# Two-layer decoder on one Trainium2 core: the expert stages' second product as three fp32r products, routing weight applied per expert behind it

## The reference

```
h1 = einsum('bth,efh->btef', x, w1) + b1;  h1 = gelu(h1)
expert_outputs = einsum('btef,ehf->bteh', h1, w2) + b2
mixed_output = sum(topk_expert_outputs * topk_weights[..., None], axis=2)
```

```
h = relu(einsum('td,edh->teh', tokens, W1) + b1[None])
y = einsum('teh,ehd->ted', h, W2) + b2[None]
out = take_along_axis(y, expert[:, None, None], axis=1)[:, 0, :];  return out * max_prob
```

## Time and profile before

| | |
|---|---|
| median of 3 runs | 1724.21 us (1723.12 to 1724.45) |
| profiled execution: span | 1721.3 us |
| stage C, from its first bias product to the first work of stage D | 806.6 to 1030.1 us |
| stage F, from its first bias product to the last transposition of `yT` | 1595.1 to 1712.3 us |
| PE busy over the span | 1529.6 us (89%) |
| DVE busy | 1183.9 us (69%) |
| ACT busy | 959.5 us (56%) |
| POOL busy | 455.7 us (26%) |

### The profile page before, as it was taken

One profiled execution on the slowest core, in us unless ns is written; L12 is line 12 of the kernel. 1 busy time (PEld: TensorE's weight loads), 2 busy tenths in 40 slices (PEclk: granted clock), 3 DMA queues, 4 the chain that ended last, 5 costly groups with the idle time before them and its releaser, 6 DMA issues.

```text
span 1721.3 us, 22204 instructions
## 1 busy us (share of the span) xinstructions
PE 1529.6 (89%) x6864; PEld 893.3 (52%) x6864; DVE 1183.9 (69%) x3060; ACT 959.5 (56%) x1953; POOL 455.7 (26%) x385
## 2 busy tenths in 40 slices
PE   5899899999989979878999998999989897786997
PEld 3455455455544355444555555666655564453554
DVE  6988788788787264676755547666665766466675
ACT  4888688678788345543444435555454542353333
POOL 2455355445445221231000002222222221111000
PEclk9999999999999999998999999999999997898999
DMA  4000000000000030001000000000000000100000
GB/s 143 1 1 1 1 1 1 1 1 1 1 1 1 0 98 1 1 1 61 1 1 1 1 12 14 1 1 1 1 1 1 1 2 0 49 1 1 1 13 13
DMA packets 13508, 18.59 MB, mean 11 GB/s; under 512 B 832, under 2 KB 9808, under 8 KB 13264
## 3 DMA queue, kind: packets, MB, share of 16 engines
q1 hardware_dynamic: 12816, 16.06, 2.9%
q10 hardware_dynamic: 576, 1.11, 0.2%
HBM read 16.11 MB, written 1.05 MB: 10 GB/s over the span
## 4 chain that ended last, share of the span: by engine, by line
PE 64%; DVE 19%; ACT 9%; issue 6%; POOL 1%; DMA 0%; ACTq 0%; POOLq 0%; DVEq 0%
PE bank L625 8%; PE bank L445 7%; PE bank L377 6%; PE bank L435 4%; PE bank L428 3%; PE bank L760 3%; PE bank L506 3%; PE bank L549 3%; PE bank L520 2%; PE bank L726 2%; PE bank L756 2%; PE bank L608 2%; PE bank L610 2%; PE bank L609 2%; DVE work L1319 2%
## 5 line engine op out<-in xcount | busy, mean ns | idle before, releaser
L1771 POOL TENSOR_TENSOR work<-work 128x512 f32<-128x512 f32 x256 | 266.2, 1040 | 285.4 <-DVE work L1327 285.4
L1069 ACT ACTIVATE work<-bank,cols 128x512 f32<-128x512 f32 x192 | 131.8, 687 | 188.0 <-PE bank L610 187.3
L904 ACT ACTIVATE work<-bank,work 128x512 f32<-128x512 f32 x256 | 176.2, 688 | 103.9 <-DVE work L1319 102.6
L1555 DVE TENSOR_TENSOR work<-work,bank 128x512 f32<-128x512 f32 x192 | 130.1, 686 | 125.1 <-ACT work L1069 123.9
L1319 DVE TENSOR_REDUCE work<-bank 128x1 f32<-128x512 f32 x256 | 175.5, 686 | 42.2 <-PE bank L429 38.9
L625 PE MATMUL bank<-work,W 128*128 128x512 f32 x384 | 198.4, 600 | 4.4 <-DVE work L1555 4.4
L435 PE MATMUL bank<-cst,work 128*128 128x128 f32 x1024 | 157.1, 277 | 30.0 <-ACT work L912 26.5
L435 PEld LDWEIGHTS bank<-cst,work 128*128 128x128 f32 x1024 | 124.4, 142 | 80.2 <-issue 45.4
L428 PE MATMUL bank<-split 128*128 128x512 f32 x256 | 156.7, 612 | 1.8 <-ACT work L904 1.4
L912 ACT ACTIVATE work<-bank 128x512 f32<-128x512 f32 x256 | 151.2, 591 | 0.7 <-PE bank L435 0.3
L445 PE MATMUL bank<-work 128*64 128x512 f32 x512 | 139.0, 623 | 0.7 <-ACT work L912 0.7
(11 more groups left out here) (223 smaller groups left out, 3086.3 us busy)
## 6 DMA issues: line engine op xcount, KB each, us to landing
W<-in_w1T SPq DMA_DIRECT2D x1, 2048.0 KB, 8.1
x_all<-in_x SPq DMA_DIRECT2D x4, 256.0 KB, 8.7
W<-in_L_attn_Wq SPq DMA_DIRECT2D x2, 512.0 KB, 4.3
W<-in_L_attn_Wv SPq DMA_DIRECT2D x2, 512.0 KB, 6.5
W<-in_L_attn_Wo SPq DMA_DIRECT2D x2, 512.0 KB, 8.6
W<-in_L_ffn_W SPq DMA_DIRECT2D x1, 1024.0 KB, 5.7
out<-x_all SPq DMA_DIRECT2D x4, 256.0 KB, 2.3
W<-in_L_attn_Wk ACTq DMA_DIRECT2D x1, 512.0 KB, 7.6
```

Of the source, the lines that this page charges most:

```text
L904: A(pA[u % 5], bank[u % 3][:, :], ACT.Exp, bias=nmax[:, u % 8:u % 8 + 1], accum_out=rsum[0][:, u % 8:u % 8 + 1]).then_inc(sem("a_e"), 1)
L1069: A(hsC[i % 3], bank[i % 3][:, :], m_["func"], bias=col(m_["b1"], s)).then_inc(sem(n + "_h"), 1)
L1555: V.tensor_tensor(hwC[i % 3], hsC[i % 3], bank[3 + (s // ft) % 2][:, :], ALU.mult)\
L1771: G.tensor_tensor(pA[u % 5], pA[u % 5], rsum[1][:, u % 8:u % 8 + 1].to_broadcast([P, S]), ALU.mult)\
```

## The change

The weight is no longer multiplied into each hidden block. A hidden block is instead split like the first operands: DVE copies it rounded to fp32r (`hiC`, four buffers), and the remainder (`loC`) is subtracted by DVE in even steps and by POOL in odd ones. `contract` makes three fp32r products in place of the plain one, one step later than before (`CLAG` = 3 steps behind `moe_h`), and accumulates one expert, not the row, in bank 3 or 4. At the end of an expert ACT adds the second bias (`ysC`), PE spreads the routing weight into bank 5, DVE multiplies the two (`accC` or `ywC`), and POOL adds the experts up; the last addition writes `yT`, which ACT did before. The bias product, the per-step multiplication and the copy of the weights for the bias product go. The second weights are split in the first row of a stage: DVE the high parts, POOL the low ones. Two small loads become columns of `cols`. The tail steps move, and entry into phase 3 waits for the last `yT`.

```diff
-        hwC, a = carve(a, S, 3)
+        ysC, a = carve(a, S, 2)
+        ywC, a = carve(a, S, 2)
...
+        accC = [wT_C[:, i * S:(i + 1) * S] for i in range(2)]
+        w2_high = split[:, 12 * S:12 * S + 4096]
+        hiC, loC = ([split[:, (20 + 4 * j + i) * S:(21 + 4 * j + i) * S] for i in range(4)] for j in range(2))
+        CLAG = 3
...
+        def wait_low(eng, m_, i):
+            name = "_lop" if i % 2 else "_lod"
+            eng.wait_ge(sem("M" + name), m_["at"][name] + i // 2 + 1)
...
+        def ends_expert(m_, i):
+            return i // m_["ft"] if i >= 0 and i % m_["ft"] == m_["ft"] - 1 and i < NB * E * m_["ft"] else None
...
-        TAIL = {0: (11, 16, 19, 19, 26), 1: (1, 3, 4, 5, 11), 2: (2, 5, 8, 11, 16), 3: (6, 7, 8, 8, 9),
-                4: (1, 3, 4, 5, 8), 5: (2, 4, 7, 7, 11)}
+        TAIL = {0: (11, 16, 19, 19, 26), 1: (1, 3, 4, 5, 11), 2: (2, 8, 11, 14, 19), 3: (6, 7, 8, 8, 9),
+                4: (1, 3, 4, 5, 8), 5: (2, 7, 10, 10, 13)}
...
-                2: [("y_ready", 12), ("C_hw", 128)],
+                2: [("y_ready", 12), ("yT_ready", 12)],
...
                 def contract(i):
-                    b, k = i // steps, i % steps
-                    if k == 0:
-                        take(pe, 5, yT_ready, m_["w0"] + b + 1)
-                        mm(bank[5][:, :], b2[:, r, :], wT_C[0:E, (b % 2) * S:(b % 2 + 1) * S], start=True, stop=False)
-                    pe.wait_ge(sem(n + "_hw"), i + 1)
-                    m = mm(bank[5][:, :], m_["w2"][:, k * D:(k + 1) * D], hwC[i % 3], start=False, stop=(k == steps - 1))
...
+                    if f == 0:
+                        where[n + "y"] = take(pe, 3 + k % 2, sem("M_ys"), m_["at"]["_ys"] + k + 1)
+                    out = where[n + "y"]
+                    if b == 0:
+                        pe.wait_ge(sem("M_ws2"), m_["at"]["_ws2"] + s // 4 + 1)
+                    wait_low(pe, m_, i)
+                    high, low = w2_high[:, s * D:(s + 1) * D], m_["low2"][:, s * D:(s + 1) * D]
+                    mm(out[:, :], high, hiC[i % 4], start=(f == 0), stop=False)
+                    mm(out[:, :], low, hiC[i % 4], start=False, stop=False)
+                    mm(out[:, :], high, loC[i % 4], start=False, stop=(f == ft - 1)).then_inc(sem("M_c"), 1)
+
+                def spread(k):
+
+                    b, e = k // E, k % E
+                    if e == 0:
+                        pe.wait_ge(sem(n + "_sel"), b + 1)
+                    out = take(pe, 5, sem("M_yw"), m_["at"]["_yw"] + k + 1)
+                    mm(out[:, :], sel[:, e:e + 1].to_broadcast([P, P]), wsel_b[b % 2], start=True, stop=True)\
+                        .then_inc(y_ready if e == E - 1 else sem("M_wb"), 1)
...
+                    if i >= CLAG:
+                        contract(i - CLAG)
+                        if ends_expert(m_, i - CLAG) is not None:
+                            spread(ends_expert(m_, i - CLAG))
...
+                    k = ends_expert(m_, i - CLAG - 1)
+                    if k is not None:
+                        act.wait_ge(sem("M_c"), m_["at"]["_c"] + i - CLAG)
+                        if k >= 2:
+                            moe_weighted(act, m_, k - 2)
+                        A(ysC[k % 2], bank[3 + k % 2][:, :], ACT.Identity, bias=col(m_["b2"], k % E)).then_inc(sem("M_ys"), 1)
+                    if b < NB:
+                        act.wait_ge(sem(n + "_hp"), i + 1)
+                        if i >= 3:
+                            wait_low(act, m_, i - 3)
+                        A(hsC[i % 3], bank[i % 3][:, :], m_["func"], bias=col(m_["b1"], s)).then_inc(sem(n + "_h"), 1)
...
+            def moe_high_w2(m_, c):
...
+                    V.tensor_copy(w2_high[:, r], m_["w2"][:, r]).then_inc(sem("M_wh2"), 1)
+
+            def moe_weigh(m_, k):
...
+                V.tensor_tensor(out, ysC[k % 2], bank[5][:, :], ALU.mult).then_inc(sem("M_yw"), 1)
...
-                V.tensor_copy(wT_C[0:E, (b % 2) * S:(b % 2 + 1) * S], src)
...
+                    k = ends_expert(m_, i - CLAG - 2)
+                    if k is not None:
+                        moe_weigh(m_, k)
...
                     if b == 0 and s % 4 == 0:
                         moe_split_w(m_, s // 4 + 2)
+                        moe_high_w2(m_, s // 4 + 2)
                     dve.wait_ge(sem(n + "_h"), i + 1)
...
-                    V.tensor_tensor(hwC[i % 3], hsC[i % 3], bank[3 + (s // ft) % 2][:, :], ALU.mult)\
-                        .then_inc(sem(n + "_hw"), 1)
+                    if i >= 4:
+                        dve.wait_ge(sem("M_c"), m_["at"]["_c"] + i - 3)
+                    high = V.tensor_copy(hiC[i % 4], hsC[i % 3])
+                    high.then_inc(sem("M_hi"), 1)
+                    if i % 2 == 0:
+                        dve.wait_ge(sem("M_hi"), m_["at"]["_hi"] + i + 1)
+                        V.tensor_tensor(loC[i % 4], hsC[i % 3], hiC[i % 4].bitcast(F32), ALU.subtract)\
+                            .then_inc(sem("M_lod"), 1)
...
+            def moe_low_w2(m_, c):
...
+                    G.tensor_tensor(m_["low2"][:, r], m_["w2"][:, r], w2_high[:, r].bitcast(F32), ALU.subtract)\
+                        .then_inc(sem("M_ws2"), 1)
...
+                        tail(m_["w0"] + b - 1, s)
+                        if i % 2:
+                            pool.wait_ge(sem("M_hi"), m_["at"]["_hi"] + i + 1)
+                            G.tensor_tensor(loC[i % 4], hsC[i % 3], hiC[i % 4].bitcast(F32), ALU.subtract)\
+                                .then_inc(sem("M_lop"), 1)
+                    k = ends_expert(m_, i - CLAG - 2)
+                    if k is not None and k % E:
+                        kb, e = k // E, k % E
+                        moe_weighted(pool, m_, k)
+                        if e < E - 1:
+                            if e >= 2:
+                                pool.wait_ge(sem("M_acc"), m_["at"]["_acc"] + (E - 2) * kb + e - 1)
+                            G.tensor_tensor(accC[kb % 2], accC[kb % 2], ywC[k % 2], ALU.add).then_inc(sem("M_acc"), 1)
+                        else:
+                            pool.wait_ge(sem("M_acc"), m_["at"]["_acc"] + (E - 2) * (kb + 1))
+                            pool.wait_ge(yt_ready, m_["w0"] + kb)
+                            G.tensor_tensor(yT[:, :], accC[kb % 2], ywC[k % 2], ALU.add).then_inc(yT_ready, 1)
```

More of the change, by code:

```diff
@@ L111, in decoder @@
         ri = sb("ri", [P, 4, 8], U32)
-        with nc.sbuf_tensor("split", [P, 12 * S], F32R) as split:
+        with nc.sbuf_tensor("split", [P, 28 * S], F32R) as split:
             pass
@@ L844, in tail @@
                 at = tail_steps(w)
-                if s == at[0] + out_pieces(w) - 1:
+                if s == at[0] + out_pieces(w) - 1 and ph not in (2, 5):
                     act.wait_ge(y_ready, w + 1)
@@ L848, in tail @@
                         act.wait_ge(yt_ready, w)
-                    src = bank[5] if ph in (2, 5) else where["y", w]
+                    src = where["y", w]
                     if ph in (1, 4):
@@ L1060, in moe @@
                 enter(act, ph)
-                for i in range(NB * steps):
+                for i in range(NB * steps + CLAG + 1):
                     b, s = i // steps, i % steps
[L1063 to L1069, removed]
+                    if b < NB:
+                        tail(m_["w0"] + b - 1, s)
+                        if s == m_["route"][1] and b + 1 < NB:
+                            moe_exp(m_, b + 1)
+                    k = ends_expert(m_, i - CLAG - 1)
[4 more added lines that the diff above has]
+                        A(ysC[k % 2], bank[3 + k % 2][:, :], ACT.Identity, bias=col(m_["b2"], k % E)).then_inc(sem("M_ys"), 1)
+                    if b < NB:
+                        act.wait_ge(sem(n + "_hp"), i + 1)
+                        if i >= 3:
+                            wait_low(act, m_, i - 3)
+                        A(hsC[i % 3], bank[i % 3][:, :], m_["func"], bias=col(m_["b1"], s)).then_inc(sem(n + "_h"), 1)
             def d_softplus(b):
@@ L1454, in moe_split_w @@
                     split_to(w1_high[:, r], m_["low"][:, r], m_["w1"][:, r]).then_inc(sem(m_["n"] + "_ws"), 1)
+            def moe_high_w2(m_, c):
+                if c < E * m_["ft"] // 4:
+                    r = slice(4 * c * P, (4 * c + 4) * P)
+                    V.tensor_copy(w2_high[:, r], m_["w2"][:, r]).then_inc(sem("M_wh2"), 1)
+            def moe_weigh(m_, k):
+                n, b, e = m_["n"], k // E, k % E
+                dve.wait_ge(sem("M_ys"), m_["at"]["_ys"] + k + 1)
+                if e == E - 1:
+                    dve.wait_ge(y_ready, m_["w0"] + b + 1)
+                else:
+                    dve.wait_ge(sem("M_wb"), m_["at"]["_wb"] + (E - 1) * b + e + 1)
+                if e == 0:
+                    out = accC[b % 2]
+                    if b >= 2:
+                        dve.wait_ge(yT_ready, m_["w0"] + b - 1)
+                else:
+                    out = ywC[k % 2]
+                    if e >= 3:
```

(40 more changed lines are left out.)

52 lines of the change are left out of this document (20 added, 32 removed).

## The result

The changed kernel takes 1781.74 us in the median of 4 runs (1777.65 to 1782.9), the one before 1723.94 (1723.12 to 1724.45): a ratio of 1.0326, 95% interval 1.0312 to 1.034. It is slower by 58 us, where 69 were forecast. The profiled execution has a span of 1775.9 us, 54.6 above that of before, and its own time was 1777.65.

The account below looks back on a forecast made before the run. PE was taken to bound the kernel before, a DVE and POOL chain after the change. Stage C +29 and F +40 us sum to +69 on the 1721.3 us span, 1790; median 1793 us, range 1748 to 1820.

Parts of the forecast that it names:

- The mechanism: Expert stages C and F: DVE's copies and subtractions take turns with POOL's operations; that chain, not PE, sets the pace.
- the walk: One expert's DVE and POOL chain followed from a copy's end: 6.04 us in C, 3.68 in F; PE needs 5.82, 3.02.
- Rival (a): DVE and POOL do not hinder each other, DVE's own work decides: 1709 us, faster; chance 0.09.
- Rival (b): The collision is there but POOL's operations cost 1.04 us, not 1.28: C +4, F +26, 1754 us; chance 0.2.
- Rival (c): As forecast, and PE, busy 65% in F, also loses its full clock: 1805 to 1820 us; chance 0.13.
- entrance: Start of stages C and F: early weight blocks fall into C's existing wait and cost nothing; spreading products only moved.
- row 0: First row of 512 tokens, with weight splitting: C 79.5 us against 59.3, +20.2; F 40.8 against 30.5, +10.
- rows 1 and 2: Middle rows, expert chain plus DVE's other work: C 58.6 us, +2.4 each; F 41.0 us, +11 each.
- row 3 and exit: Last row and the serial exit through POOL, ACT and DVE: C 55.3 against 51.7, +4; F 34.5 against 26.6, +8.
- the wait of 7.99 us: Wait at stage C's start, assumed to stay and absorb earlier weight blocks; were it gone, 8 us more.
- the 11.6 us of other work: DVE's routing, splitting and normalising in a row of F, lengthening the chain at its new steps; 11.2 us in C.
- PE's gain: Three fp32r products for the plain one, eight bias products gone: some 36 us if PE stayed the bound; C's row 50.5.

Follow-up runs that it names:

- pool_short: Changed kernel with POOL's odd-step subtractions and its additions cut to 8 of 512 columns, output not the reference's: 1715.21 us, 0.9944 of before.
- sel_first: Changed kernel with PE's wait for the routing weights put back ahead of the previous stage's last output product: 1786.01 us, 1.0353 of before.
- hi_on_act: Changed kernel with ACT making the rounded high part by a second activation, DVE all low parts and no copies, POOL only adding: 1737.01 us, 1.0071 of before.
- before_early_out: Kernel before with only the last output product ahead of an expert stage moved before PE's wait for the routing weights: 1717.24 us, 0.9956 of before.
- pool_writes: Changed kernel with POOL's odd-step subtraction replaced by two memsets that read nothing: 1745.71 us, 1.0122 of before.

## Why the prediction was right, and where its terms were off

**The mechanism** held in every step that was tested. DVE and POOL take turns (1.66 and 1.14 us for operations of 0.69 and 0.42), and that chain sets the pace: an expert of C took 6.07 us against 6.04 in the walk, one of F 3.68 against 3.68, rows 59.2 against 58.6 and 39.46 against 41.0. Rival (a), no hindrance, is what pool_short shows on purpose: 1715 us, where the rival had said 1709. Rival (b), POOL at 1.04 us, was wrong: POOL's subtraction never took less than 1.26.

**Rival (c), the clock.** In F the granted clock did fall, to 0.91 in the mean of the row shown. What it cost is not separable here, but with DVE busy for 37.76 of 39 us little time is left for it.

**The terms.** Measured from the first block's product to the first work behind the stage: stage C took 1030.16 - 788.91 = 241.3 us before and 1050.69 - 788.39 = 262.3 after, +21.0, where +29 was forecast. Stage F took 132.87 before (1579.46 to 1712.33) and 167.45 after (1599.20 to 1766.65), +34.6, where +40 was forecast. Stages D and E between them took 0.8 us less. The rest of the 54.6 is the earlier start of C, 0.5 us the other way, and 0.3 us more behind F's last transposition.

ACT's activation of step 2 of a row tells where in a stage the time went: before, it starts 0.04 us behind the bias product by which the prediction dated the rows. In rows 0, 1 and 3 of stage C after:

```profile
799.60 0.69 ACT L1103 ACTIVATE work<-bank,cols 128x512 f32<-128x512 f32 x1
...
876.99 0.69 ACT L1103 ACTIVATE work<-bank,cols 128x512 f32<-128x512 f32 x1 [0.71 <-PE bank L630]
...
995.31 0.69 ACT L1103 ACTIVATE work<-bank,cols 128x512 f32<-128x512 f32 x1 [0.71 <-PE bank L630]
```

The same marks in F, in the kernel before and in sel_first give this table of what each part cost more than before, in us:

| | C forecast | C measured | C in sel_first | F forecast | F measured | F in sel_first |
|---|---|---|---|---|---|---|
| entrance: first block to step 2 | 0 | -6.6 | -0.7 | 0 | -5.7 | -2.3 |
| row 0 | +20.2 | +18.1 | +15.0 | +10 | +13.0 | +10.7 |
| rows 1 and 2 | +4.8 | +5.8 | +5.9 | +22 | +18.8 | +18.8 |
| row 3 and exit | +4 | +3.7 | +3.7 | +8 | +8.4 | +8.4 |

The largest mis-sized term is the entrance, 12.3 us in both stages together. The walk began at the old place of step 2, 806.6 us, as if the wait of 7.99 us stayed and only took in the early weight blocks. I had read the diff's new place of the spreading product as "only moved" and costed it at nothing; its wait moved with it, past the output product. Step 2's products started 9.9 us after the stage's first block in place of 16.4, and the wait of 7.99 us was gone. The prediction had said "were it gone, 8 us more"; the entrance became shorter instead, and some of that came back in row 0.

sel_first, with the wait put back, shows how much: row 0 is then 3.1 us shorter in C and 2.3 in F, so 2.9 us of C and 1.1 of F hang on that wait in the end. It also sizes row 0 from the place where the walk began. In F the +10.7 agree with the forecast. In C they are +15.0 for +20.2: my placing of layernorms, weight blocks and POOL's three operations added up too much by some 5 us. Which of them is not settled.

In F rows 1 and 2 cost +9.4 each where +11 was forecast. Since the bare chain of an expert is 3.68 us as forecast, the miss is in the 11.6 us of other work: eight experts leave 39.46 - 29.4 = 10.0 for it, so some 1.5 us more than I placed were hidden beside POOL. Those 11.6 us and the 11.2 of C were given without their working, and the row of F in rival (a) adds up to 30.4, not 29.9, when its parts are taken from the row durations; neither changes an outcome.

**PE's gain** was forecast at 56.2 - 50.5 = 5.7 us a row of C; with PE at 49.00 of 49 us in pool_short it is 6.9.

## What to carry to other kernels

Before work is given to an idle POOL, look for a place in the trace where POOL and DVE run at once and read what DVE's copies and two-input SBUF operations take there: here the idle engine was free in the busy table and cost 66 us in the chain. DVE's multiplication with an operand in PSUM (0.67 us beside POOL) and ACT's rounding from the bank (0.68 us in the mean beside POOL in hi_on_act) escaped it. With the rounding on ACT the fp32r products paid in stage C, 51.4 us a row for 56.2, and not in stage F, 36.7 for 30.06, where an expert has only two steps and PE waits for the weighting. And when an instruction is moved, its wait moves too: ask what now passes ahead of it.

## What the runs showed of the hardware that was not expected

The last output product's sixteen matmuls take 7.03 us in before_early_out, where the granted clock is 1.00 from 791.4 to 798.2, and 9.52 in the kernel before, where it is 0.72 from 796.4 to 805.4 (PE, PEld, DVE, ACT, POOL, granted clock):

```profile
791.40:798.20 6.80, 6.80 (x18) 2.93 (x17) 5.48 (x10) 0.25 (x1) 0.00 (x0) 1.00 0.00 0
796.40:805.40 9.00, 9.00 (x18) 3.81 (x16) 2.92 (x6) 0.00 (x0) 0.00 (x0) 0.72 0.01 2
```

Part of the second stretch is at the lower of the two levels, 1.2 GHz, after PE had waited 3.54 us for DVE. That wait was followed by 2.5 us more for the product, so it was paid some 1.7 times. The changed kernel and sel_first show the same pair, 7.03 and 9.94 us.

In pool_writes POOL's memset, which reads nothing, left DVE's subtraction at 0.69 us but was itself stretched from 0.52 to 0.76 by DVE's copy.
